# Writing out the last stage of a four-stage transformer kernel, and moving transfers and routing steps of its first two stages

## The reference

```python
x = x + moe_a(layernorm(x), ctx)     # 8 experts, 128->512->128, relu; top 2 by ctx @ Wg + bg, softmax of the two
x = x + moe_b(layernorm(x))          # 16 experts, 128->128->128, silu(W1 x) * (W3 x); sigmoid scores,
                                     # 2 of 4 groups, then top 4 in them, weights * 2.5 / sum
x = x + attention(layernorm(x), ctx) # 16 heads of 8, strictly causal mask, softmax, Wo and bias
y = layernorm(x)                     # the last stage, on y itself:
h = layernorm(y) * gamma + beta      # a second normalisation
x = x + y + 0.5 * (silu(h @ fc1 + b1) @ fc2 + b2)   # 128 -> 512 -> 128, weights dequantised from integers
```

## Time and profile before

| | us |
|---|---|
| median of three runs | 939.17 |
| the three runs | 939.17, 939.89, 934.89 |
| the profiled execution, its time | 934.4 |
| its span, from first to last instruction | 932.6 |

### The profile page before, as it was taken

The page is one execution under the profiler, slowest core; times in us unless marked ns, Lnnn a source line. Parts: engine busy times, 40 slices in busy tenths (PEclk is TensorE's granted clock), DMA queues, the critical chain, the costliest instruction groups (busy, mean ns, idle before and its releaser), DMA issues.

```text
span 932.6 us, 18423 instructions
## 1 busy us (share of the span) xinstructions
PE 799.3 (86%) x5525; PEld 608.4 (65%) x5580; DVE 643.1 (69%) x1911; ACT 504.1 (54%) x972; POOL 400.3 (43%) x461
## 2 busy tenths in 40 slices
PE   3369898999994998988599899789999999987886
PEld 3358687899973787866388688545555555545564
DVE  6758564456676476868467576597888887847886
ACT  2435454567752566764266466445555555555664
POOL 6233776067102737430467730246765433441111
PEclk9999899999998899998799899899999999997888
DMA  9931488563112228112124220134544464420101
GB/s 307 352 103 60 136 254 245 196 199 103 53 35 87 58 80 300 59 35 63 40 65 135 69 48 25 56 96 132 144 141 117 125 167 130 121 59 4 30 22 34
DMA packets 96153, 104.56 MB, mean 112 GB/s; under 512 B 13401, under 2 KB 71145, under 8 KB 94780
## 3 DMA queue, kind: packets, MB, share of 16 engines
q1 hardware_dynamic: 76994, 79.72, 27.0%
q0 software_dynamic: 8608, 18.22, 7.7%
q10 hardware_dynamic: 10464, 5.51, 2.0%
HBM read 67.17 MB, written 36.23 MB: 111 GB/s over the span
## 4 chain that ended last, share of the span: by engine, by line
PE 38%; issue 14%; POOL 7%; DVE 7%; DMA 1%; ACT 1%; DVEq 0%; POOLq 0%; ACTq 0%
PE y_ps L1996 3%; PE y_ps L1909 3%; PE hid_ps L1972 3%; PE hid_ps L1973 2%; PE hid_ps L1984 2%; PE hid_ps L1894 2%; POOL xr L625 2%; PE tr_ps L2055 2%; POOL yg L633 2%; PE hid_ps L1877 2%; PE tr_ps L2027 1%; PE y_ps L290 1%; PE y_ps L1911 1%; PE hid_ps L1879 1%; PE y_ps L292 1%
## 5 line engine op out<-in xcount | busy, mean ns | idle before, releaser
L625 POOL DMA_INDIRECT xr<-b_tokens,idx_sb x70 | 66.7, 953 | 114.4 <-DVE idx_sb L901 94.1
L1120 DVE TENSOR_TENSOR hl<-hid_ps,hh 128x512 fp32r<-128x512 f32 x78 | 53.8, 690 | 69.3 <-ACT hh L1484 68.3
L1282 DVE TENSOR_REDUCE negmax<-hid_ps 128x4 f32<-128x512 f32 x128 | 85.9, 683 | 11.2 <-PE hid_ps L1973 10.5
L1783 PE MATMUL y_ps<-region,hh 128*128 x312 | 83.6, 345 | 10.7 <-DVE hl L1120 10.4
L633 POOL DMA_INDIRECT yg<-a_rows,idx_a x64 | 61.0, 954 | 50.3 <-issue 50.3
L1229 DVE TENSOR_TENSOR zb<-hid_ps,sg 128x256 f32<-128x256 f32 x70 | 29.7, 424 | 73.8 <-ACT sg L1568 51.9
L655 POOL DMA_INDIRECT yg<-b_rows,idx_b x64 | 61.0, 954 | 44.1 <-DMA b_rows<-yo 26.7
L1478 ACT ACTIVATE zb<-hid_ps 128x512 f32<-128x512 f32 x78 | 46.4, 595 | 60.5 <-PE hid_ps L1763 60.3
L1562 ACT ACTIVATE sg<-hid_ps 128x512 f32<-128x512 f32 x70 | 41.7, 596 | 67.4 <-PE hid_ps L1879 60.6
L1909 PE MATMUL y_ps<-region,hh 128*128 x280 | 75.4, 347 | 0.6 <-DVE hl L1240 0.6
L1973 PE MATMUL hid_ps<-region 128*128 128x512 f32 x128 | 75.2, 589 | 0.0
(11 more groups left out here) (338 smaller groups left out, 2420.7 us busy)
## 6 DMA issues: line engine op xcount, KB each, us to landing
region<-k_strips SPq DMA_DIRECT2D x128, 64.0 KB
region<-k_strips SPq DMA_DIRECT2D x32, 256.0 KB, 2.9
region<-hl SPq DMA_DIRECT2D x128, 64.0 KB
k_strips<-k_halves SPq DMA_DIRECT2D x24, 256.0 KB
region<-nought SPq DMA_DIRECT2D x6, 1024.0 KB
a_rows<-yo SPq DMA_DIRECT2D x20, 256.0 KB
b_rows<-yo SPq DMA_DIRECT2D x18, 256.0 KB
staged<-a_w_in SPq DMA_DIRECT2D x16, 256.0 KB, 6.2
```

The source lines that it names most:

```text
L625: g.indirect_dma_start(xr[:, q % 3, j * RB:j * RB + w], None, src, bass.IndirectOffsetOnAxis(ap=rows.bitcast(U32), axis=0)).then_inc(x_got ...
L1282: v.tensor_reduce(negmax[:, s % 2, b, :], hid_ps[b % 2][:].rearrange("p (i k) -> p i k", i=HG), AX, ALU.max, negate=True).then_inc(c_max, 1)
L1783: t.matmul(y[:, c0:c0 + 2 * P], hh[:, n % 2, cs], w2a[:, bass.ds(e * (2 * FA) + c * 2 * P, 2 * P)], start=c == 0, stop=False)
```

## The change

- Stage D is written out block by block without loops. The statistics of blocks 0 to 6 (`stats_d`) are made in attention's ticks 22, 23, 25, 26, 28, 29 and 32 (`DST`), their roots one tick later (`power_d`), block 7's within D's first block. The halving goes from DVE to ACT (`halve`), with the halved bias `b2h` made in tick 25. PE makes the next block's up products 0 and 1 between the down products 1 and 2. The transposes back go to `cb_ps` instead of `tr_ps`.
- The four loads of the second half of x go from ACT's queue (L1461) to SP's, behind a wait for the first gathered slots; the zero fills stand behind them. The 2 MB store into `k_img` goes behind the first stored rows.
- `scatter_a(4)` stands behind `power` 6 and 7, and `gather_a(2)` ahead of the roots of blocks 0 and 1.
- The tables of A and B: every routing step of the first tuple from `SGM` on comes three steps sooner, `SLT` 35 for 38; of the second tuple one to four sooner, `SLT` 31 for 33, `CMB` 3, 7, 11, 15 for 7, 11, 15, 19. The table store of a half waits at `WTS` + 1 on ACT.
- Keys and values two steps later, B's weight splits every fourth step for every third; the routing of the second half of A spread over more steps (`find_a` apart).

```diff
-        CMB = ((7, 11, 16, 21), (7, 11, 15, 19))
-        STT = ((8, 12, 17, 22), (8, 12, 16, 20))
-        APP = ((10, 14, 19, 23), (9, 13, 17, 21))
+        CMB = ((6, 9, 13, 18), (3, 7, 11, 15))
+        STT = ((7, 10, 14, 19), (4, 8, 12, 16))
+        APP = ((11, 13, 17, 20), (7, 11, 15, 17))
...
-            (26, 24), (27, 25), (28, 25), (28, 26), (31, 26), (29, 28), (33, 29), (34, 30), (37, 33), (36, 32), (38, 33))
+            (23, 20), (24, 22), (25, 23), (25, 24), (28, 23), (26, 25), (30, 27), (31, 28), (34, 31), (33, 30), (35, 31))
...
-        KAT, VAT = [4 * i + 7 for i in range(NB)], [4 * i + 9 for i in range(NB)]
+        KAT, VAT = [4 * i + 9 for i in range(NB)], [4 * i + 11 for i in range(NB)]
+        DST = (22, 23, 25, 26, 28, 29, 32)
...
-            return 3 * c + 2 if c < 10 else SA + 3 * c - 28
+            return 4 * (k - NRAW_A) + 3
...
+            sp.wait_ge(x_got[0], 16 * NT)
+            for b in range(BH, NB):
+                sp.dma_start(X[:, b * BT:(b + 1) * BT].rearrange("p (t d) -> p t d", t=NT),
+                             x[b * BT:(b + 1) * BT, :].rearrange("(t p) d -> p t d", p=P)).then_inc(in_x[BH], 16)
             sp.wait_ge(cleared, 2)
...
-                    pool.wait_ge(logits_a, NH2)
+                    pool.wait_ge(kv_mm, 2 * NB)
...
-            scatter_a(4)
             power(6, 7)
             power(7, 8)
+            scatter_a(4)
...
+            gather_a(2)
             power(0, NB + 1)
-            gather_a(2)
             power(1, NB + 2)
...
-                if T == WTS[h]:
+                if T == WTS[h] + 1:
                     eng.wait_ge(wts_ready, h + 1)
...
+            def halve(b):
+                eng.wait_ge(d_down, CD * (b + 1))
+                a.activation(accT[:, b % 2, :], y_ps[b % 2][:], ACT.Identity, bias=b2h[:, 0:1], scale=0.5).then_inc(acc_ready, 1)
...
+            for b in range(NB):
+                if b + 1 < NB:
+                    apply_d(b + 1)
+                low_d(b, 0)
+                residual(b)
+                low_d(b, 1)
+                if b + 1 < NB:
+                    low_x(b + 1)
+                write_back(b - 1)
+                low_d(b, 2)
+                low_d(b, 3)
...
+            for b in range(NB):
+                up_d(b, 2)
+                up_d(b, 3)
+                if b + 1 < NB:
+                    eng.wait_ge(xn_ready, NB + b + 2)
                     fwd()
+                down_d(b, 0)
+                back_d(b - 1)
+                down_d(b, 1)
+                if b + 1 < NB:
+                    up_d(b + 1, 0)
+                    up_d(b + 1, 1)
+                down_d(b, 2)
+                down_d(b, 3)
+            back_d(NB - 1)
```

More of the change, by code:

```diff
@@ L759, in _ @@
                     pool.wait_ge(rstd_ready, C0 + b + 1)
+                for b in range(NB - 1):
+                    if tau == min(DST[b] + 1, STEPS - 1):
+                        power_d(b)
                 if -4 <= tau < 12:
@@ L764, in _ @@
                     gather_b(BH + (tau + 4) // SG, 2 * i, 2 * i + 2)
-            def rstd_step(stage, i, p):
-                pool.wait_ge(var_ready, at(stage, i, p, 1, 2))
-                g.tensor_tensor(rstd[:], veps[:], mhalf[:], ALU.pow).then_inc(rstd_ready, 1)
-            with pool.Fori(0, NB // 2) as i:
-                for p in range(2):
-                    rstd_step(STAGE_D, i, p)
+            power_d(NB - 1)
         def ln_stats(eng, link, off):
@@ L1171, in _ @@
                 h, T = divmod(n, SA)
+                q, j = group_a(n)
+                last = n == SA - 1
+                if last:
+                    rows_out(q, j, pair_of(group_a, n)[0], a_yc, pair_of(group_a, n)[0] + 1, a_y)
                 if n + 1 < NA:
                     low_a(n + 1)
-                q, j = group_a(n)
-                if ends_pair(n, SA):
+                if ends_pair(n, SA) and not last:
                     rows_out(q, j, pair_of(group_a, n)[0], a_yc, pair_of(group_a, n)[0] + 1, a_y)
@@ L1318, in _, with stats_d @@
             v.tensor_tensor(bo, bo, y_ps[0][:, 0:1], ALU.add).then_inc(bv_done, 1)
+            def stats_d(b):
+                for t in range(NT):
+                    ins = v.bn_stats(st[:, t, :], X[:, b * BT + t * P:b * BT + (t + 1) * P])
+                link(ins)
+                v.memset(carry[:], 0.0)
+                for t in range(NT):
+                    ins = v.bn_aggr(d_mv[:, b, t, :], st[:, t, :])
+                link(ins)
+                link(v.tensor_scalar_add(d_veps[:, b, 0, :], d_mv[:, b, :, 1], EPS))
+                v.scalar_tensor_tensor(d_veps[:, b, 1, :], d_veps[:, b, 0, :], EPS, d_mv[:, b, :, 1],
+                                       op0=ALU.mult, op1=ALU.add).then_inc(var_ready, 1)
             for tau in range(-5, STEPS + 3):
@@ L1458, in _ @@
             table_a(3)
-            eng.wait_ge(logits_a, 1)
-            for b in range(BH, NB):
-                load_x(b)
             for k in range(8, NRAW_A):
@@ L1529, in _ @@
                 h, T = divmod(n, SA)
+                q, j = group_a(n)
+                last = n == SA - 1
+                if last:
+                    rows_half(q, j, pair_of(group_a, n)[0], a_down, n + 1, a_yc)
                 if n + 2 < NA:
@@ L1831, in _ @@
                 h, T = divmod(n, SA)
+                if n == SA - 1:
+                    down_a(n)
                 if n + 2 < NA:
@@ L1841, in _ @@
                     background(0, T)
-                for i in range(NB if h == 0 else 0):
+                for i in range(NB):
                     b, u = KVB[i], (i + 2) % 4 * BT
-                    if T == KAT[i]:
+                    if n == KAT[i]:
                         if i >= 2:
```

253 lines of the change are left out of this document (127 added, 126 removed).

## The result

The changed kernel takes 896.72 us (median of 4 runs, 890.41 to 901.64) beside 939.53 for the kernel before (4 runs on the same chip, 934.89 to 940.38): a ratio of 0.955, 95% interval 0.948 to 0.962. It is faster, by 42.8 us in the medians. The prediction said 876, range 858 to 900. The time is inside the range of 8 in 10 and outside the forecast's own 866 to 888; the sum promised 58.6 us where 37.0 came.

What follows compares the result with a forecast made beforehand. It took PE as the bound where nothing interrupts it, with time lost in a few places of waits and low clock. Terms summed to 58.6 us: 934.4 - 58.6 = 875.8, likeliest 876, range 858 to 900 for 8 in 10.

Steps and rivals of the forecast that it cites:

- Start: Kernel start: first gather and x no longer wait behind table stores and zero fills; 8 us saved, bounds 3.4 and 10.5.
- A's first half: Stage A, first half: root wait at T = 11 gone 7.5, expert search split 2, weight wait 4 us saved.
- Moving keys and values two steps changes no work: 0: Stage A, first half: keys and values moved two steps, costed at 0 us.
- A's second half: Stage A, second half: root behind gathers loses 6 us at T = 11, weights give 1.5; together a 4.5 us loss.
- Passage to B: From A to B: slot list three steps sooner removes PE's 8.33 us wait; 9.5 us saved, bounds 6 and 11.
- B's first half: Stage B, first half and its passage: slots wait 4, ACT's weights wait 4.5, sooner list 7; together 15.5 us saved.
- Attention: Attention ticks: seven groups of D's statistics put into DVE's free time; 1 us lost, bounds -1 and +5.
- Stage D: Stage D: 7.6 us a block plus 4.5, 65.3 for 83 us; 17.6 us saved, bounds 9.7 and 22.5.
- SP's queue: Rival: late fills on SP's in-order queue delay weights throughout A's first half; 940 us or more, chance 0.03.
- The gathers do set the pace: Rival: POOL's gathers set the pace of A and B, gains return as row waits at `CMB`; 901 us, chance 0.18.
- D had its full clock in the middle, so that rival fell: Rival: stage D keeps its clock, at 8.6 us a block; 884 us, chance 0.12.
- three signs of being wrong: Gathers' rows late at `CMB`, D's low parts still ending PE's waits, or fills holding up the weights.

Runs made afterwards that it cites:

- the three together: Changed kernel with keys and values one step sooner, group 5's slots ahead of block 4's scatters, D's statistics in ticks 28 to 34; 885.77 us, ratio 0.946.
- B's old table: Changed kernel with the steps of B's first half, from combining to routing, as in the kernel before; 1076.06 us, ratio 0.981, on a disturbed chip.
- D alone: Kernel before with only stage D and attention's ticks as in the changed kernel; 916.63 us, ratio 0.978.
- the run with group 5 sooner: Changed kernel with the gathers of group 5's slots ahead of block 4's eight scatters on POOL; 1074.87 us, ratio 0.980, on a disturbed chip.

## Why the prediction came out as it did

- **Start** (8): right, 7.7. The list is there at 34.11, the gathers run at once, and the rows are used 1.7 us after the last issue of the group ends. By the Trainium skill (DMA: Bandwidth & Descriptors, section SWDGE vs HWDGE vs iDMA) a DMA engine goes round its internal queues in turn; the prediction drew 8.5 from it. The short landing agrees, and no run here tells the two sums apart.
- **A's first half** (13.5, got 4.7): the waits that were to go are gone: 12.2 us by step 16, where 9.5 were promised (8.0 of it the root, 4.2 in steps 1 to 12 against the 2 of the expert search), and 4.3 at step 28 for 4. Two steps of the working failed. "The scatters still start no later" looked at the scatters and not at the gathers of slots that the roots' new place puts behind them: 6.8 us. "Moving keys and values two steps changes no work: 0" priced the instructions and not the queue on which their stores stand: 6.3.
- **A's second half** (-4.5, got -10.8): the size of the loss at T = 11 was right (6 predicted, 6.6 in steps 50 and 51), its cause was not. It is the row wait at T = 9 (2.93), the root's is 0.38. "Combining fits the pace of the gathers to about 1 us" failed: the combining comes two steps sooner, and the gathers start 2.8 us later, behind the last values, which moved by two steps. So one edit that was costed at nothing took 6.3 us in one half and 2.7 at the border, and has a share in the 6.6 of the other. The experiments with keys and values one step sooner show the first directly. The share in the second is argued from the trace and not shown: in the three together the gathers start as late, and the table with the old steps for combining was not run.
- **Passage to B** (9.5, got 5.9): right mechanism, wrong size. Three steps were counted at 2.8 us, but PE's last three steps of A take 2.3, 1.8 and 1.3; the last two have no up products of a later step to make. The list comes 5.9 us sooner against the last step (4.2 ahead of it for 1.7 behind), and a wait of 2.42 stays.
- **B's first half** (15.5, got 10.7): the passage gave 8.1 for 7 and m = 12 gave 3.3 for 4; ACT's wait gave 2.6 for 4.5. The term that is missing is -3.6 in steps 13 to 29: the routing stands closer together on DVE, and PE waits 7.7 us for its low parts where it waited 2.6. B's old table brings back both the passage and the shorter steps.
- **Attention** (-1, got -4.1): "DVE is free for 1.2 us a tick" is a mean; the statistics come in one piece ahead of a part that PE needs. That makes 3.2 us of waits, and 1.5 of low clock behind the last of them; a hole of 1.7 comes on top, and 1.7 are given back where block 0's statistics left. It was inside the bounds, at their poor end. D alone shows the same loss, and the hole stays when the statistics go to the tail.
- **Stage D** (17.6, got 22.8): the forecast for the new stage was met, 65.3 us, by luck: the period was overrated (6.7 for 7.6) and the way in and out underrated by as much. The base was off: 83 us is the window of the earlier trace rows, which leaves out the first block's way in and the last one's way out; from D's first transposes to the end the kernel before takes 88.1. Where the gain comes from was measured in part: 11.9 to 12.6 us the order on PE, 3.1 to 3.8 the statistics of five blocks out of D, 1.0 to 1.7 the halving on ACT. Each was taken back alone, and in none did the clock in D's middle leave 1.00, though PE's shorter busy time makes about half of the gain. What brought it back, and what going without the hardware loops is worth by itself, no run shows. By the Trainium skill (TensorE: Matmul & The Clock Gate, section HAM oscillation) feeding the array without gaps keeps it from falling back to its low clock; the trace agrees, clock 1.00 in D's middle. That the 22.5 drawn from it is near the 22.8 is chance: with 7.0 a block D would have taken 60.5 us, and it took 65.3.
- **The rivals.** SP's queue did become late, but through the stores of values and not through the fills, and at 6.3 us and not 59. The gathers do set the pace at one place in A. The time of that rival (901) is nearer to the 896.7 than the forecast's 876, and the cause of most of the difference is another: the two orders of POOL's and SP's queues. D had its full clock in the middle, so that rival fell. Of the prediction's three signs of being wrong one came, rows late at `CMB`.
- **Luck and slips.** Seven of the nine places came out poorer than forecast, by 27.4 us in all, and D gave 5.2 more than promised, for a reason that was not foreseen. Without those 5.2 the time would have been 902, outside the range. Two sums are off by little: eight gathers at 1.25 us from 210.71 end at 220.7, not 220.9, and 83 less 65.3 is 17.7, not 17.6.

## What to carry to other kernels

Cost a moved step at every queue that it enters, and in that queue's own units: a store that is put behind "the rows of its group" moves by a whole group when its step crosses a border, and a load behind it moves as well. Ask of each edit costed at nothing what starts when it ends; here the last values free a buffer, and the gathers of the next stage begin there. Take a stage's length from its own first and last instruction, not from the round window in which its rates were read. And before an edit's step is called mended, look at the same step in a neighbour without the edit: the one beside the run with group 5 sooner was as short.

## What was not expected of the hardware

- On two of the three chips of the experiments the kernel before took 1096.5 us for 935.8, with the same instructions: DVE was busy for 632.7 us in the kernel with keys and values sooner, and for 632.5 in the changed one on the first chip, yet PE, DVE and ACT stood still in the first for 81, 102 and 39 us with no releaser, up to 17 us at a time, and nearly all of it ahead of attention. What holds them was not found.
- A hole of this kind of 1.7 us sits in score tick 23 of the changed kernel on both good chips and, with 1.6, in the one with stage D alone, not in the kernel before. It stays with the statistics in the tail (2.1 and 1.1 us), and six of the eight kernels on the disturbed chips lack it. The profile has a queue of instructions (q8), of packets of 16 KB. Of the changed kernel's DMA from 746.5 to 748.5 us, with the hole from 747.1 to 748.8:

```profile
q8 instruction: 1, 0.02, 3.0%
```

In all fourteen traces one such packet starts near the end of score tick 23. Where it starts 0.7 to 1.2 us before PE has ended the tick (the kernel before and those six) there is no hole; where it starts at most 0.4 us before that end, or up to 1.0 behind it (the other seven), PE stands still for 1.1 to 2.1 us. So the supply of instructions fits this hole in every trace; no run changed that supply alone, so it is not shown as the cause. The long holes of the disturbed chips mostly have no such packet beside them.
